# Local attention with a ternary feed-forward layer: output bias as a rank-one TensorE product, remote bias later on GpSimd, output products behind all query-key products, another order of the prologue

## The reference

```
qkv = x @ qkv_w + qkv_b
local = local_attention(q, k, v)                  # window 128, softmax
pooled = mean of x over chunks of 8;  rkv = pooled @ rkv_w + rkv_b
remote = softmax(rq . rk, chunks before own) @ rv @ rout_w + rout_b
gate = sigmoid(local @ gl_w + remote_h @ gr_w)
mixed = gate * local + (1 - gate) * remote_h
y = layernorm(x + mixed @ out_w + out_b)
out = layernorm(y + ternary(gelu(ternary(y, w_up)), w_down))
```

## Time and profile before

| What | us |
|---|---|
| Median of 3 runs (range) | 1233.28 (1229.51 to 1234.33) |
| The profiled execution's own time | 1231.08 |
| Its span, first to last instruction | 1229.3 |
| PE busy | 998.9 |
| DVE busy | 925.4 |
| POOL busy | 743.4 |
| ACT busy | 697.9 |
| Mean granted TensorE clock, as a share | 0.931 |

### The profile page before, as it was taken

One profiled execution on the slowest core, in us unless ns is written; L12 is line 12 of the kernel. 1 busy time (PEld: TensorE's weight loads), 2 busy tenths in 40 slices (PEclk: granted clock), 3 DMA queues, 4 the chain that ended last, 5 costly groups with the idle time before them and its releaser, 6 DMA issues. The chain is left out here.

```text
span 1229.3 us, 36825 instructions
## 1 busy us (share of the span) xinstructions
PE 998.9 (81%) x15240; PEld 637.4 (52%) x15240; DVE 925.4 (75%) x1836; ACT 697.9 (57%) x1125; POOL 743.4 (60%) x915
## 2 busy tenths in 40 slices
PE   4768887988889798888979788897878888794855
PEld 2445564645556464555646455564645556463433
DVE  6578787886868788686878868687887867786444
ACT  2424665646566564646666465665657466663644
POOL 7125674665667466566846656674665667564664
PEclk9879998999999899999989999998999999996787
DMA  6750514215051422505142250514225050421000
GB/s 185 195 143 12 147 38 140 70 62 147 29 146 38 138 72 70 139 29 147 38 142 67 69 140 29 147 38 138 72 69 141 28 147 21 138 55 35 2 18 18
DMA packets 58867, 107.43 MB, mean 87 GB/s; under 512 B 20518, under 2 KB 38726, under 8 KB 55622
## 3 DMA queue, kind: packets, MB, share of 16 engines
q1 hardware_dynamic: 58556, 105.08, 30.3%
q10 hardware_dynamic: 144, 0.00, 0.0%
HBM read 70.87 MB, written 33.55 MB: 85 GB/s over the span
## 5 line engine op out<-in xcount | busy, mean ns | idle before, releaser
L853 ACT ACTIVATE Pt<-scores 128x1024 f32<-128x1024 f32 (+1 forms) x256 | 229.8, 918 | 130.4 <-PE oacc L1543 84.2
L691 POOL TENSOR_TENSOR h_lo<-hbuf,h_hi 128x512 f16<-128x512 f32 x128 | 148.2, 1158 | 182.3 <-DVE h_hi L1252 182.3
L1125 DVE TENSOR_REDUCE nmax<-work 128x3 f32<-128x480 f32 x352 | 214.9, 633 | 33.8 <-PE work L1494 30.5
L663 POOL TENSOR_SCALAR_AFFINE_SELECT Pt<-Pt 128x512 f32<-128x512 f32 x256 | 165.3, 646 | 55.6 <-ACT Pt L853 55.3
L650 POOL TENSOR_TENSOR parts<-Pt,parts 128x512 bf16<-128x512 f32 x64 | 73.0, 1160 | 159.5 <-ACT parts L781 159.4
L1543 PE MATMUL oacc<-Pt,Vp 128*32 128x256 f32 (+1 forms) x2048 | 153.9, 361 | 14.8 <-POOL Pt L667 9.2
L1489 PE MATMUL work<-Ks,Qs 98*32 98x160 bf16 x4096 | 146.2, 236 | 16.0 <-DVE nmax L1125 7.1
L1252 DVE CAST h_hi<-hbuf 128x512 f16<-128x512 f32 x128 | 68.1, 532 | 115.7 <-ACT hbuf L889 115.3
L1520 PE MATMUL scores<-Qs,Ks 100*32 100x160 bf16 (+4 forms) x4096 | 120.0, 230 | 34.4 <-ACT Pt L853 17.4
L1520 PEld LDWEIGHTS scores<-Qs,Ks 100*32 100x32 bf16 x4096 | 82.3, 98 | 81.4 <-ACT Pt L853 51.5
L1382 PE MATMUL scores<-xT,wqk 128*128 128x512 f32 x256 | 118.7, 608 | 6.2 <-DMA xT<-x_t 6.2
(11 more groups left out here) (169 smaller groups left out, 1992.8 us busy)
## 6 DMA issues: line engine op xcount, KB each, us to landing
parts_scratch<-parts SPq DMA_DIRECT2D x96, 256.0 KB, 5.1
Qs<-parts_scratch SPq DMA_DIRECT2D x96, 256.0 KB, 4.8
Ks<-parts_scratch SPq DMA_DIRECT2D x96, 256.0 KB, 5.0
xT<-x_t SPq DMA_DIRECT2D x16, 512.0 KB, 3.9
xres<-x SPq DMA_DIRECT2D x16, 512.0 KB, 4.6
y<-nat SPq DMA_DIRECT2D x16, 512.0 KB, 3.0
Qs<-nmax_pair SPq DMA_DIRECT2D x256, 2.0 KB, 1.8
nat<-up_t SPq DMA_DIRECT2D x1, 1024.0 KB, 5.9
```

What stands on the lines that cost most here:

```text
L663: ins = pool.affine_select(out=pt[:, :, 0:P], in_=pt[:, :, 0:P], compare_op=ALU.is_gt, fill=0.0, base=0, pattern=[[0, 4], [1, P]], channel ...
L691: pool.tensor_tensor(h_lo[:, t % NR, :], hbuf[:, t % 2, :], h_hi[:, t % NR, :], ALU.subtract).then_inc(h_lo_ready, 1)
L853: nc.scalar.activation(Pt[:, u % NPT, :, 0:w], scores[:, slot, :, :].rearrange("p k (h q) -> p (k h) q", h=2)[:, :, 0:w], ACT.Exp, scale=S ...
L1125: nc.vector.tensor_reduce(nmax[:, first:first + n], work[:, slot, 0:n * BAND].rearrange("p (h c) -> p h c", h=n), X, ALU.max, negate=True) ...
```

## The change

- The output bias is no longer added by POOL. In the prologue DVE splits it into three bf16 rows of a tile `bout_rows` (partitions 0, 32 and 64, zeros elsewhere), and PE adds it in the accumulation of the output product, by a product of all-ones bf16 weights `ones_b` with `bout_rows`: two more products at each of `OUT` and `OUT+1`. DVE waits for the residual's DMA itself.
- `bias_remote(s.next())` moves on POOL to the end of step `XN_HI`, behind `x1`.
- `OUT` moves behind `QK+3` in `SECOND_HALF`. On ACT alone the tanh of `GATE` is done behind the step `QK`.
- Prologue: the weights count on three semaphores (`w_lat`, `w_val`, `w_in`) and are issued in another order; preparing constants is split off and moved to a step `CONSTANTS` behind sequence 0's `LAT_T`; all of sequence 1's remote path now lies between the maxima of sequence 0, ahead of `T`.

```diff
 SECOND_HALF = (
-    ("F", GATE), ("P", QK), ("P", QK + 1), ("P", QK + 2), ("F", OUT), ("P", QK + 3),
-    ("F", OUT + 1), ("P", LAT_RQ), ("P", LAT_RKV), ("P", VALUES), ("P", LAT_SCORES), ("F", NORM),
+    ("F", GATE), ("P", QK), ("P", QK + 1), ("P", QK + 2), ("P", QK + 3), ("F", OUT), ("F", OUT + 1),
+    ("P", LAT_RQ), ("P", LAT_RKV), ("P", VALUES), ("P", LAT_SCORES), ("F", NORM),
...
+GATE_AT = ("P", QK)
...
-    order += [("P", 0, LAT_T), ("P", 0, LAT_T + 1)]
+    order += [("P", 0, LAT_T), ("P", 0, LAT_T + 1), ("W", 0, CONSTANTS)]
...
-    between = {1: ("P", 0, REMOTE), 3: ("P", 0, REMOTE + 1), 5: ("P", 1, VALUES), 8: ("P", 1, VALUES + 1),
-               17: ("P", 1, LAT_SCORES), 19: ("P", 1, LAT_EXP), 20: ("P", 1, LAT_EXP + 1)}
+    between = {1: [("P", 0, REMOTE)], 3: [("P", 0, REMOTE + 1)], 5: [("P", 1, VALUES)], 7: [("P", 1, LAT_SCORES)],
+               9: [("P", 1, LAT_EXP)], 10: [("P", 1, LAT_EXP + 1)], 12: [("P", 1, VALUES + 1)],
+               13: [("P", 1, LAT_NORM), ("P", 1, LAT_NORM + 1)], 14: [("P", 1, VALUES + 2)],
+               16: [("P", 1, LAT_T), ("P", 1, LAT_T + 1)], 17: [("P", 1, VALUES + 3)], 18: [("P", 1, LAT_O)],
+               20: [("P", 1, REMOTE), ("P", 1, REMOTE + 1)]}
...
-    order.append(("T", 0, 0))
-    order += [("P", 1, k) for k in (LAT_NORM, LAT_NORM + 1, VALUES + 2, VALUES + 3)] + [("W", 0, TERNARY)]
-    return order + [("P", 1, k) for k in (LAT_T, LAT_T + 1, LAT_O, REMOTE, REMOTE + 1)]
+    return order + [("T", 0, 0), ("W", 0, TERNARY)]
...
@@ POOL, f_step at XN_HI, and body
+                    if s.next().exists and not s.first:
+                        bias_remote(s.next())
...
-                for b in range(NB):
-                    add_bias(s, b)
-                if s.next().exists and not s.first:
-                    bias_remote(s.next())
@@ ACT, body
-                    if phase == "F":
+                    if phase == "F" and k != GATE:
                         f_step(s, k)
-                    elif later.exists:
+                    elif phase == "P" and later.exists:
                         p_step(later, k)
-                    if s.i == B - 2 and (phase, k) == ("F", GATE):
+                    if (phase, k) == GATE_AT:
+                        f_step(s, GATE)
+                    if s.i == B - 2 and (phase, k) == GATE_AT:
@@ DVE, prepare_constants
+                for k in range(3):
+                    row = slice(k * GT, k * GT + 1)
+                    for j in range(k + 1):
+                        link(nc.vector.tensor_copy(bout_rows[row, :], bout[row, :]))
+                        if j < k:
+                            link(nc.vector.tensor_tensor(bout[row, :], bout[row, :], bout_rows[row, :], ALU.subtract))
@@ DVE, f_step at OUT
-                        dve.wait_ge(xres_done, count(s, NB, NB - 1))
+                        dve.wait_ge(xres_in, count(s, 1, 0) * 16)
@@ PE, f_step at OUT
                     for b in range(2 * c, 2 * c + 2):
-                        mm = product(work[:, slot, (b % 2) * D:(b % 2 + 1) * D],
-                                     lambda t: mixT[:, c, t, (b % 2) * P:(b % 2 + 1) * P], lambda t: wout[:, t, :])
+                        o = work[:, slot, (b % 2) * D:(b % 2 + 1) * D]
+                        for t in range(KT):
+                            nc.tensor.matmul(o, mixT[:, c, t, (b % 2) * P:(b % 2 + 1) * P], wout[:, t, :],
+                                             start=(b % 2 == 0 and t == 0), stop=False, skip_group_check=True)
+                    for b in range(2):
+                        mm = nc.tensor.matmul(work[:, slot, b * D:(b + 1) * D], ones_b[:, :], bout_rows[:, :],
+                                              start=False, stop=True, skip_group_check=True)
                     mm.then_inc(w_full[slot], 1)
```

More of the change, by code:

```diff
@@ L271, in build @@
         bout = sb("bout", [P, D])
+        bout_rows = sb("bout_rows", [P, D], BF16)
+        ones_b = sb("ones_b", [P, P], BF16)
         glb = sb("glb", [P, HD])
@@ L332, in build @@
         bqk_in = sem("bqk_in")
+        w_lat = sem("w_lat")
+        w_val = sem("w_val")
         w_in = sem("w_in")
@@ L450, in build @@
             (brv[:, :], rows_of_all(rkv_b[LD:2 * LD], LD)),
+        ]
+        val_loads = [
             (wv[:, :, :, :].rearrange("p t h d -> p t (h d)"), v_w.rearrange("(t p) n -> p t n", p=P)),
+            (glb[:, :], rows_of_all(gl_w, HD)),
+        ]
+        loads = [
+            (nat[0].rearrange("p (t f) -> p t f", t=KT), up_t.rearrange("(t p) f -> p t f", p=P)),
+            (nat[1].rearrange("p (t d) -> p t d", t=FT), down_t.rearrange("(t p) d -> p t d", p=P)),
+            (wqk[:, :, :], qk_w.rearrange("(t p) n -> p t n", p=P)),
+            (wout[:, :, :], out_w.rearrange("(t p) n -> p t n", p=P)),
+            (wro[0:LD, :], rout_w),
+            (wro[LD:2 * LD, :], rout_w),
             (bv_col[:, :], bass.AP(v_b.tensor, v_b.offset, [[1, P], [P, KT]])),
@@ L552, in _ @@
                 load_x(Seq(0, 0, 0))
+                for dst, src in lat_loads:
+                    sp.dma_start(dst, src).then_inc(w_lat, 16)
+                for dst, src in val_loads:
+                    sp.dma_start(dst, src).then_inc(w_val, 16)
                 for dst, src in loads:
@@ L601, in _ @@
             link(pool.memset(wrog[:, :], 0.0))
+            link(pool.memset(bout_rows[:, :], 0.0))
+            link(pool.memset(ones_b[:, :], 1.0))
             pool.sem_inc(consts, 1)
@@ L722, in bias_remote @@
                 ins.then_inc(rem_biased, 1)
-            def add_bias(s, b):
-                if b == 0:
-                    pool.wait_ge(xres_in, count(s, 1, 0) * 16)
-                if b == 0 and s.first:
-                    pool.wait_ge(bias_ready, 1)
-                pool.tensor_tensor(xres[:, b, :], xres[:, b, :], bout[:, :], ALU.add).then_inc(xres_done, 1)
             def finish_before(s):
@@ L916, in w_step @@
             def w_step(j):
-                if j == EDGES:
+                if j == CONSTANTS:
                     act.wait_ge(gate_bias, 1)
@@ L971, in prepare @@
                 nc.vector.tensor_tensor(rem_b[:, :, :], rem_b[:, :, :], bv_q[:, :, :], ALU.subtract)
-                dve.wait_ge(gate_bias, 1)
-                link(nc.vector.tensor_tensor(bout[:, :], bout[:, :], oacc[:, 0, 0:D], ALU.add))
-                dve.sem_inc(bias_ready, 1)
-                for w3, o in [(wv[:, t, :, 0:HD], wv[:, t, :, HD:VN]) for t in range(KT)]:
-                    link(nc.vector.tensor_tensor(tmp, w3, gl3, ALU.mult))
-                    link(nc.vector.tensor_reduce(o, tmp, X, ALU.add))
+                wro3 = wro[:, :].rearrange("p (h d) -> p h d", h=H)
+                gr3 = grb[:, :].unsqueeze(1).to_broadcast([P, H, HD])
                 link(nc.vector.tensor_tensor(tmp, wro3, gr3, ALU.mult))
@@ L998, in w_step @@
                 if j == PREP:
-                    prepare()
+                    prepare_values()
+                if j == CONSTANTS:
+                    prepare_constants()
                 if j == TERNARY:
@@ L1664, in _ @@
                             pe.wait_ge(prep_done, 1)
+                        if k == REMOTE + 1:
+                            pe.wait_ge(prep_done, 2)
                         if k == LAT_SCORES:
```

38 lines of the change are left out of this document (18 added, 20 removed).

## The result

The changed kernel takes 1181.35 us (median of four runs, 1179.26 to 1185.92) against 1233.74 us (1229.51 to 1234.33) of the kernel before on the same chip: a ratio of 0.9587, with a 95% interval from 0.9552 to 0.9623. The forecast was 1178, the range 1168 to 1202.

A forecast was written before the change was run, and what follows sets the result against it. Bound: the chain through DVE's stretched gate and the detour over the fourth query-key product, not PE. Sum: -13 x 4.3 - 0.9 + 3 = -53.8 against 1231.08 gives 1177.3, stated as 1178 us; range 1168 to 1202.

The forecast's parts named there:

- Gate, 2.6 us of stretches: DVE's gate chain in the second half: three small instructions stretched by POOL's two biases lose 0.62 + 1.01 + 0.96 us.
- The rival that the change turns slower by the tanh: ACT's tanh waits behind the first query-key copy for a late product, delaying all that follows: 1258 us, chance 0.03.
- PE's wait and the slow output product: PE's 3.14 us wait for DVE's mix is filled; the first output product takes 1.89 us, not 3.36.
- Bias products: Four on PE per sequence, about 0.15 us each, 0.6 in all; covered because the first output bank fills before DVE takes it.
- 15.2 us from line 1177 to the last statistics: Second half of sequence 7: gate to DVE's last layer-norm statistics takes 15.2 us, not 18.9; 4.3 us won per sequence.
- My lower bound: Least gain per sequence in the second half, 2.3 us, with two variance steps stretched by 1.0 us each.
- Sequences 14 and 15: No query-key work there: 0.6 us of gate won, four bias products paid; zero together, bounds -1.5 and +2.
- The collisions move along: POOL's third parts now collide with DVE's variances: 2.3 us won per sequence, prologue 7, 1207 us; chance 0.17.
- Remote bias in 2 us of slack: On POOL it ends at 636.5, before the first remainder is due at 638.5, so it costs nothing.
- DMAs of the maxima: They keep their place and become the bound, leaving 2.5 us won per sequence: 1201 us; chance 0.05.
- Prologue, +3: Sequence 1's remote path, 6.28 us of PE, moves ahead of the split; 3.5 us of idle absorbs part: 3 us charged.
- All that follows moves with it: Everything behind DVE's last statistics comes earlier by the same 4.3 us per sequence.

The follow-up runs named there:

- The last two experiments: Changed kernel, old prologue, holes filled, early tanh: POOL's last third part behind the last statistics, 1154.72 us; then also the remote bias halved between feed-forward remainders, 1154.43 us.
- the holes filled: Changed kernel with the old prologue, two value products moved on PE alone into its waits around the layer norm's transposes: 1157.41 us, ratio 0.9411.
- the order alone: Kernel before, its only edit the output products moved behind all four query-key products; POOL keeps both biases: 1208.51 us, ratio 0.9812.
- the old prologue: Changed kernel with sequence 1's remote path finished behind the split of the maxima again; semaphores and weight issue order stay changed: 1173.97 us, ratio 0.9554.
- the bias out of the prologue: Changed kernel with sequence 1's remote bias moved from the prologue to the end of step XN_HI of sequence 0: 1183.75 us, ratio 0.9623.

## Why the prediction was right, and where it was not

- **The sum:** the forecast was 53.8 us, the medians differ by 52.4. By the ledger the fourteen ways gave 2.3 us less than forecast, the prologue cost 2.6 more and the rest 4.1 more, all in one direction (the end gave back 0.3); the traced execution is the slowest of its four. So that 1178 lies within 4 us of 1181.35 owes something to luck.
- **Gate, 2.6 us of stretches:** right to the hundredth: lines 1195, 1198 and 1203 take 0.23, 0.26 and 0.29 us in sequence 7. The tanh came 0.2 us late, as charged; the run with it in front showed that this is all it costs. The rival that the change turns slower by the tanh is thereby excluded.
- **PE's wait and the slow output product:** gone, as forecast. Bias products: charged 0.15 each and covered; they take about 0.11 and are covered, for DVE takes the first output bank about 2 us behind them (603.96), as I had it.
- **15.2 us from line 1177 to the last statistics:** measured 609.54 - 594.39 = 15.15. Per sequence 4.3 were forecast. In eleven sequences it was 4.1 to 4.4; in two the way had been 19.0 and lost 3.0. I had read one sequence and multiplied by thirteen: 53.5 us in place of 55.9. (My lower bound was off too: two variance steps stretched by 1.0 each, in place of the 0.4 charged, give 4.3 - 1.6 = 2.7, not 2.3.) Sequence 0: 1.0 for 0.9. Sequences 14 and 15: a ledger of -0.3 for 0.
- **The collisions move along** (first rival): they did, but to places with a small price. Line 1250 is stretched to 0.48 us in its first use (0.3 us, of 0.4 charged), line 1257 to 1.11 as before, and in the prologue the split pays 1.3 us. The last two experiments show that the rival is right as a warning: one further removal met a full queue on POOL, the next one another collision.
- **Remote bias in 2 us of slack:** covered, as forecast. In sequence 7 only 0.9 us are to spare: it ends at 617.9, and POOL waits 0.88 us for the first remainder at 618.79. But sequence 7 is the one with the full clock in this stretch, where the feed-forward layer comes earliest; in the other twelve of sequences 1 to 13 POOL waits 2.0 to 2.9 us. With the holes filled the slack is 0.9 in nearly all, and there it did run out when the third part was moved.
- **DMAs of the maxima** (second rival): refuted. Their issue begins at 622.43 and the scores start at 637.68, 15.25 us behind it, as before (646.43 to 661.69); all of it moved with the chain.
- **Prologue, +3:** the term that was mis-sized, +5.4 to the first scores in this pair of traces and near 7 over all profiles of either prologue. I let 3.5 us of PE's idle time ahead of the split take up the moved work; it took none: the stretch from the first maxima to the split grew from 22.4 to 28.0 us, and PE's idle in it from 3.5 to 5.7. The 12 us behind the split were the DMAs of the maxima all along, so emptying PE there bought nothing, and the collision added 1.3. The maxima start 1.5 us earlier than before in this pair; but the order alone, with the prologue of the kernel before, starts them earlier still (49.2 us), so nothing shows that the earlier weights did it.
- **"All that follows moves with it"** was off by 4.1 us over fourteen sequences in this execution. I looked at the clock only at the output product. PE's holes between the transposes stayed, and behind them the clock fell further than before in seven sequences, at about 0.7 us each. It is not a fixed price of the change: the same second half with the old prologue has a rest of 721.9 us, as the kernel before had (721.8), and with the bias out of the prologue 724.4. That these holes cost clock, and the clock time, is shown by filling them and by the table of sequences; why it falls further here than before the change is not. The old order in the changed kernel (0.82 in thirteen sequences, never below) and the new order alone on the kernel before (0.65 to 0.69 in seven) speak for the order; but the changed kernel with the old prologue has the new order too, and was below 0.82 in two sequences only and at 1.00 in four. With the bias out of the prologue seven are below 0.82 again, without the bias products four, with the tanh in front three. That stays open: only single profiles stand behind each count.

## What to carry to other kernels

Where DVE and GpSimd collide, price the blocked DVE instruction by what is left of the other's instruction, however short it is itself (here it ended up to 0.1 us behind it), and look at what the blocked one's chain meets at each place to which the work could go; a bias product on a matrix engine that is ahead anyway cost nothing in fourteen of the sixteen sequences here. When waits are shortened on one chain, read the granted clock in the stage behind as well: small holes that seem harmless can cost a lower clock for microseconds, and moving independent products into them on that engine alone can be worth as much as removing a collision (here 17 us with four lines). Before moving work ahead of a transfer, ask whether the time behind it was ever more than the time that the transfer takes.

## What the runs showed that I had not expected

- Two PE waits of 1.1 to 1.3 us, with a microsecond of transposes between them, went before a fall of the clock in thirteen of fourteen sequences: in sequence 1 of the changed kernel the mean of 9.6 us is 0.65, near the lower of the two levels (1.2 of 2.4 GHz). In sequence 7, with waits of nearly the same length, it is 1.00, so one sequence of one profile says little about the clock. With both waits filled it was 1.00 in thirteen of fourteen sequences.
- POOL's additions block a DVE instruction with two SBUF inputs until they end (1.25 us in place of 0.23) and leave the reciprocal, with one, at its usual 0.55.
- The gain of a reordering depended on what else was there: 2.0 us per sequence with the collisions, 0.6 without.
